# Next batch's norm, and the queries' half of its first projection and rotation, moved ahead of the second norm's columns

## The reference, cut to what matters

```python
x = x + attn(layernorm(x), Wq, Wk, Wv, Wo, lambda_*)   # x: (16, 1024, 256)
x = x + ffn(layernorm(x), ...)

def attn(x):                       # 16 half-heads of 16 columns, 8 value heads of 32
    q, k = rope(x @ Wq.T) * scaling, rope(x @ Wk.T)
    v = x @ Wv.T
    probs = softmax(einsum('bhtd,bhsd->bhts', q, k))
    diff = probs[:, :, 0] - lam * probs[:, :, 1]
    a = einsum('bhts,bhsd->bhtd', diff, v)
    a = a * rsqrt(mean(a * a) + 1e-05) * (1.0 - LAMBDA_INIT)
    return a @ Wo.T

def ffn(x):                        # a recurrence from batch to batch, c carried along
    def step(c, xt):
        ft = sigmoid(xt @ wf.T + c @ uf.T + bf)
        it = sigmoid(xt @ wi.T + c @ ui.T + bi)
        gt = tanh(xt @ wc.T + c @ uc.T + bc)
        return ft * c + it * gt
    c_final = scan(step, c0, x)
    return tanh(x @ wo.T + c_final @ uo.T + bo)
```

## Time and profile before

| what | us |
|---|---|
| median of 3 runs | 5033.72 (5031.82 to 5034.27) |
| the profiled execution, its own time | 5053.02 |
| its span, first to last instruction | 5051.2 |
| PE busy in it | 4895.6 (97%) |
| DVE busy | 3960.6 (78%) |
| POOL busy | 2930.4 (58%) |
| ACT busy | 2884.9 (57%) |

### The profile page before, as it was taken

The page is one execution under the profiler, slowest core; times in us unless marked ns, Lnnn a source line. Parts: engine busy times, 40 slices in busy tenths (PEclk is TensorE's granted clock), DMA queues, the critical chain, the costliest instruction groups (busy, mean ns, idle before and its releaser), DMA issues.

```text
span 5051.2 us, 67243 instructions
## 1 busy us (share of the span) xinstructions
PE 4895.6 (97%) x24784; PEld 1745.4 (35%) x24784; DVE 3960.6 (78%) x6295; ACT 2884.9 (57%) x5221; POOL 2930.4 (58%) x2134
## 2 busy tenths in 40 slices
PE   7999999999999999999999999999999999999999
PEld 2224242332424233242332424233242433324237
DVE  7888878888887878878887887888788787887526
ACT  1565646656465665646566464665646566564642
POOL 3583837657374674728567383764738477472740
PEclk7899999999999999999999999999999999999999
DMA  6121222303122130222313123230312313022117
GB/s 151 30 56 52 47 66 53 66 32 66 47 47 72 34 76 38 55 59 47 72 34 62 46 47 70 48 66 30 67 48 47 72 34 76 39 47 55 68 51 291
DMA packets 127867, 311.19 MB, mean 62 GB/s; under 512 B 27313, under 2 KB 30514, under 8 KB 113714
## 3 DMA queue, kind: packets, MB, share of 16 engines
q1 hardware_dynamic: 124562, 289.72, 24.1%
q10 hardware_dynamic: 2976, 17.17, 0.9%
HBM read 172.07 MB, written 99.61 MB: 54 GB/s over the span
## 4 chain that ended last, share of the span: by engine, by line
PE 77%; POOL 11%; ACT 5%; DVE 3%; issue 3%; DMA 0%; SPq 0%; ACTq 0%; DVEq 0%; POOLq 0%
PE s_ps L795 15%; PE o_ps L835 15%; PE st L822 14%; PE st L928 13%; POOL pair_sum L484 11%; PE sum_ps L850 7%; PE st L763 4%; PE st L781 4%; ACT probs L591 3%; DVE neg_max L1127 2%; PE st L1005 2%; PE st L906 1%; PE o_ps L750 1%; DVE xa L1114 1%; PE s_ps L1005 1%
## 5 line engine op out<-in xcount | busy, mean ns | idle before, releaser
L484 POOL TENSOR_TENSOR pair_sum<-probs 128x512 f32<-128x512 f32 x2048 | 2822.1, 1414 | 1211.3 <-ACT probs L591 1210.6
L1127 DVE TENSOR_REDUCE neg_max<-s_ps 128x1 f32<-128x512 f32 x4096 | 2582.1, 682 | 700.2 <-PE s_ps L795 697.8
L591 ACT ACTIVATE probs<-st 128x512 f32<-128x512 f32 x4096 | 2162.3, 603 | 971.6 <-PE st L822 810.6
L795 PE MATMUL s_ps<-k_stack,q_stack 96*128 96x512 bf16 x4096 | 1523.0, 389 | 43.5 <-DVE neg_max L1127 37.0
L822 PE MATMUL st<-q_stack,k_stack 99*128 99x512 bf16 x4096 | 1475.8, 385 | 28.7 <-ACT probs L591 7.5
L835 PE MATMUL o_ps<-probs,values 128*32 128x512 f32 x8192 | 1095.3, 607 | 12.2 <-ACT probs L591 8.5
L822 PEld LDWEIGHTS st<-q_stack,k_stack 99*128 99x128 bf16 x4096 | 368.3, 97 | 1360.1 <-ACT probs L591 905.2
L795 PEld LDWEIGHTS s_ps<-k_stack,q_stack 96*128 96x128 bf16 x4096 | 400.7, 98 | 686.0 <-DVE neg_max L1127 336.6
L850 PE MATMUL sum_ps<-pair_sum,ones 128*32 128x512 f32 x4096 | 534.9, 594 | 26.6 <-POOL pair_sum L484 26.6
L928 PE MATMUL st<-pair_sum,weights 128*128 128x512 f32 x768 | 381.9, 594 | 11.8 <-ACT pair_sum L547 11.8
L541 ACT ACTIVATE probs<-st,gate_bias 128x512 f32<-128x512 f32 x192 | 131.7, 686 | 441.7 <-PE st L928 441.7
(11 more groups left out here) (151 smaller groups left out, 2926.6 us busy)
## 6 DMA issues: line engine op xcount, KB each, us to landing
q_stack<-qk_parts SPq DMA_DIRECT2D x384, 128.0 KB, 4.3
k_stack<-qk_parts SPq DMA_DIRECT2D x381, 128.0 KB, 7.0
swapped<-xa SPq DMA_DIRECT2D x128, 256.0 KB, 2.4
qk_parts<-swapped SPq DMA_DIRECT2D x64, 512.0 KB, 2.8
qk_parts<-low_part SPq DMA_DIRECT2D x64, 256.0 KB, 3.0
probs<-in_x SPq DMA_DIRECT2D x16, 1024.0 KB, 9.7
x_rows<-probs SPq DMA_DIRECT2D x16, 1024.0 KB, 3.9
xa<-in_x SPq DMA_DIRECT2D x15, 1024.0 KB, 6.0
```

Source lines behind the costliest of these rows:

```text
L484: pool.tensor_tensor(pair_sum[q % 2][:, h, :], probs[a % 4][:, h, :], probs[(a + 1) % 4][:, h, :], ALU.add)\
L591: act.activation(probs[kk % 4][:, h, :], st[n % BANKS][:, :], ACT.Exp).then_inc(exp_done, 1)
L795: pe.matmul(s_ps[i % BANKS][:, :], q_stack[g][0:SROWS, s, t * P:(t + 1) * P], k_stack[g][0:SROWS, s, h * HALF:(h + 1) * HALF], start=True, ...
L1127: dve.tensor_reduce(neg_max2[:, at, i % 2:i % 2 + 1], s_ps[i % BANKS][:, :], AX.X, ALU.max, negate=True).then_inc(max_done, 1)
```

## The change

With "following" for a batch b < NB - 2, that is, one in whose iteration batch b+2's first unit is prepared:

- The next norm's eight `bn_stats` go from the end of the batch into steps 26 to 31 of the odd attention, the seven small operations behind its last step. POOL makes the scales before those of the second norm.
- ACT applies the norm right behind the last mean square's reciprocal root, in two halves, each with its `take_xt`. PE transposes half 0 in front of `WO` tile 2 and half 1 in front of tile 3.
- PE projects the queries (two tiles) behind `WO` tile 3 and before the first gate. ACT takes them before the second norm's columns. SP swaps them behind the store of x2 and stores the parts before `shift_rows`.
- DVE makes rotation steps 0, 1, 2, 4, 6 between the last 15 maxima of `LATE` (`ROPE_BESIDE`), behind the second norm's second half. ACT makes casts 3 and 5 in front of gates 1 and 3.
- The second norm's transposes of half 0 go in front of the third gate's cell half, and `turn_max` in front of gate 6.
- The keys' two tiles come at the end of the iteration, all eight scores beside them (1, 1, 2, 4), and only the keys' rotation is left in the even attention, in steps 1, 2, 4, 6, 9. `score_plan` counts both moves.
- Before the loop POOL rotates unit 2 as well, so the first attention has no rotation.
- The slots of the ring are counted anew. What is computed stays the same.

```diff
+FIRST_QK0, FIRST_QK1, FIRST_VAL, NEXT_QK0, PRE = 0, 4, 8, 12, 16
+QK1, WO, QK0, GATE, QK0_LAST, GEE = 0, 12, 16, 18, 30, 32
...
-ROPE_AT = ({1: 0, 2: 1, 3: 2, 4: 7, 5: 8, 6: 4, 7: 9, 9: 6, 13: 11, 16: 13},
+ROPE_AT = ({1: 7, 2: 8, 4: 9, 6: 11, 9: 13},
            {5: 0, 6: 1, 7: 2, 8: 7, 9: 8, 10: 4, 12: 9, 13: 6, 16: 11, 20: 13})
-CAST_AT = ({4: 3, 7: 5, 11: 10, 14: 12}, {9: 3, 12: 5, 14: 10, 18: 12})
+CAST_AT = ({5: 10, 7: 12}, {9: 3, 12: 5, 14: 10, 18: 12})
+ROWS_AT = {26: (0, 1), 28: (2, 3), 29: (4,), 30: (5, 6), 31: (7,)}
+ROPE_BESIDE = ((0, 1), (1, 2), (2, 5), (4, 5), (6, 2))
...
+ROW_WORK = 0.6
...
+    WORK[1][s] += ROW_WORK * len(ROWS_AT.get(s, ()))
...
@@ sync
                 if not last:
                     if b > 0:
-                        swap(u + 2, 0, ab)
-                    store_parts(u + 2)
+                        swap_part(u + 2, 1, slot(b - 1, QK0_LAST + 1))
+                        store_part(u + 2, 1)
                     stack(u + 2, 0, 0)
...
                 sp.dma_start(x2_scr[b, :, :], x2).then_inc(x2_out, 16)
+                if b < NB - 2:
+                    swap_part(u + 4, 0, slot(b, QK0 + 1))
...
+                if b < NB - 2:
+                    store_part(u + 4, 0)
+                if not last:
                     shift_rows(u + 2, 0)
...
-            swap(2, 0, act_base(0, False))
+            swap(2, NEXT_QK0)
             shift_rows(0, 0)
+            store_parts(2)
@@ gpsimd
+                if b < NB - 2:
+                    next_scales(b)
                 for h in range(2):
                     inv_sqrt_half(b, h)
-                if b < NB - 2:
-                    next_scales(b)
...
+            rope(2)
             for b in range(NB - 1):
                 iteration(b, False)
@@ scalar
+                if following:
+                    for h in range(2):
+                        normalise_next(b, range(4 * h, 4 * h + 4))
+                        take_xt(own(b) - 1, xt, (h,))
+                    take_half(0, slot(b, QK0))
+                take_xt(own(b), xt2, (0,))
+
+                casts = {(0, 0, 1): (3,), (0, 1, 0): (5,)}
...
                         for a, func in enumerate((ACT.Sigmoid, ACT.Sigmoid, ACT.Tanh)):
-                            if b < NB - 2 and (h, m, a) == (1, 1, 2):
-                                take_xt(own + 1, xt, (1,))
+                            if following:
+                                for step in casts.get((h, m, a), ()):
+                                    part_of(2 * b + 4, step)
...
                 if not last:
                     act.preload_act_table_set("natural_log_exp_and_others")
+                if following:
+                    take_half(1, slot(b, QK0_LAST))
@@ tensor
-                rows_out(WO, W_O, attn_t, b, ab, js=(2, 3))
+                if following:
+                    transposes(xa, ln1_out, b + 2, own(b) - 1, halves=(0,))
+                rows_out([slot(b, WO + 2)], W_O, attn_t, js=(2,))
+                if following:
+                    transposes(xa, ln1_out, b + 2, own(b) - 1, halves=(1,))
+                rows_out([slot(b, WO + 3)], W_O, attn_t, js=(3,))
+                if following:
+                    pe.wait_ge(xt_out, 4 * own(b))
+                    project(0, 0, slot(b, QK0))
...
                 for i in range(BANKS):
-                    turn(GATE + i, b, ab)
+                    if i == BANKS - 1:
+                        transposes(xn2, ln2_out, b, own(b), halves=(0,))
+                    turn(slot(b, GATE + i))
                     gate_part(i, True, True, False)
...
-                    if i == 5 and not last:
-                        turn_max(u + 2)
                     if i == 6:
-                        pe.wait_ge(xt_out, 4 * own + 4)
-                    if i in (9, 11) and b < NB - 2:
-                        transposes(xa, ln1_out, b + 2, own + 1, halves=(i // 11,))
+                        pe.wait_ge(xt_out, 4 * own(b) + 4)
+                        if not last:
+                            turn_max(u + 2)
...
-                if b < NB - 2:
-                    pe.wait_ge(xt_out, 4 * (own + 2))
+                if following:
+                    project(1, 0, slot(b, QK0_LAST),
+                            ((u + 3, 1, i) for i in range(BEFORE, BEFORE + BESIDE)), (1, 1, 2, 4))
+                elif not last:
+                    for i in range(BEFORE, BEFORE + BESIDE):
+                        score(u + 3, 1, i)
@@ vector
                         rope(turned, [ROPE_AT[g][s]])
+                    if following is not None and s in ROWS_AT:
+                        dve.wait_ge(x_in, 16 * (following + 1))
+                        norm_rows(xa, ROWS_AT[s])
...
-                attention(u, 0, u + 1, PLAN0, None if last else u + 2)
+                attention(u, 0, u + 1, PLAN0, u + 2 if 0 < b and not last else None)
...
-                          None if last else u + 3)
+                          None if last else u + 3, b + 2 if following else None)
+                if following:
+                    norm_stats(b + 2, -0.5)
...
-                maxima(u + 2, late, LATE[3])
                 normalise_half(b, 1, x2, xn2)
+                for step, n in ROPE_BESIDE:
+                    if following:
+                        rope(u + 4, (step,))
+                    maxima(u + 2, late, n)
                 if not last:
-                    maxima(u + 2, late, LATE[4])
                     join_max(u + 2)
-                    if b < NB - 2:
-                        dve.wait_ge(x_in, 16 * b + 48)
-                        norm_stats(b + 2, xa, -0.5)
                     split_shift(u + 2)
```

More of the change, by code:

```diff
@@ L181, in ring @@
             return st[n % BANKS][:, :]
-        tail_ps = [ring(ring_base(NB - 1, True) + GEE + j) for j in range(3)] + [s_ps[2][:, :]]
+        tail_ps = [ring(slot(NB - 1, GEE + j)) for j in range(3)] + [s_ps[2][:, :]]
         first_in = sem("first_in")
@@ L249, in build, with own @@
         block = ctx.enter_context(nc.Block())
-        def act_base(b, last):
-            return b * ACT_ITER + (PRE - (PRE if last else 0))
+        def own(b):
+            return 2 * b + (3 if b < NB - 2 else 2 if b == NB - 2 else 1)
         def flat(buffer):
@@ L275, in value, with swap_part, swap @@
                 return v if isinstance(v, int) else sp.lower_val(v)
-            def swap(u, g, ab):
-                first = isinstance(u, int) and u == 0
-                raw_out = [value(ab + (QK1 if g else QK0) + 2 * X + 2) for X in range(2)]
-                for X in range(2):
[L283 to L288, removed]
+            def swap_part(u, X, n):
+                sp.wait_ge(act_out, taken(n))
+                if u > 0:
+                    sp.wait_ge(parts_out[X], 32 * u)
+                for a in range(2):
+                    sp.dma_start(swapped[a:P:2, X, :], raw[X][1 - a:P:2, :])\
+                      .then_inc(swap_in[X], 16)
+            def swap(u, first):
+                for X in range(2):
+                    swap_part(u, X, first + 2 * X + 1)
             def store_part(u, X):
@@ L554, in take_qk, with take_v @@
                         act.wait_ge(rope_done, 2 * u - 1 + X)
[L555 to L561, removed]
+                    take_half(X, first + 2 * X)
+            def take_v(slots, js):
+                for n, j in zip(slots, js):
+                    take(n, values[:, 2 * j:2 * j + 2, :].rearrange("p a b -> p (a b)"))
             def copy_o(u, g, r):
@@ L637, in iteration @@
                     if not last and i == 2:
-                        take_v(rb, VAL, (2, 3))
-                own = 2 * b + (1 if last else 2)
-                take_xt(own, xt2, (0,))
+                        take_v([slot(b, VAL[j]) for j in (2, 3)], (2, 3))
                 def normalise_next(b, ts):
@@ L677, in take_first @@
                 act.wait_ge(rope_done, X + 1)
-                for h in range(2):
-                    take(0, QK1 + 2 * X + h, raw[X][:, h * HALF:(h + 1) * HALF])
+                take_half(X, FIRST_QK1 + 2 * X)
             for step in (3, 5):
@@ L874, in iteration @@
             def iteration(b, last):
-                ab = act_base(b, last)
                 u = 2 * b
-                if not last:
-                    if b > 0:
-                        qk(0, b, ab, ((u + 1, 1, i) for i in range(BEFORE, sum(EARLY))),
-                           (1, 1, 0, 0, 1, 1, 2, 2))
-                    pe.wait_ge(act_out, ab + QK0 + 4)
-                else:
-                    for i in range(BEFORE, sum(EARLY)):
-                        score(u + 1, 1, i)
-                    pe.wait_ge(act_out, ab + PRE)
+                following = b < NB - 2
+                pe.wait_ge(act_out, taken(slot(b, LAST_RMS[0] if last else QK1) - 1))
                 attention(u, 0, u + 1, PLAN0)
@@ L985, in _ @@
             turn_max(0)
-            for i in range(sum(EARLY)):
+            for i in range(BEFORE + BESIDE):
                 score(1, 1, i)
```

232 lines of the change are left out of this document (119 added, 113 removed).

## The result

| | us |
|---|---|
| kernel before, median of 4 | 5033.58 (5031.82 to 5034.27) |
| changed kernel, median of 4 | 5065.56 (5064.42 to 5069.43) |
| ratio | 1.0064, interval 1.0052 to 1.0076 |
| profiled execution after, its own time and span | 5069.43, 5067.6 |

The account below looks back on a forecast made before the run. PE's own work was taken to bound the kernel, so only waits that PE feels count. Terms sum to +0.15 us a batch, +2 over 14, 0 with the first batch, on 5033.7: 5033 us, range 5010 to 5056.

Parts of the forecast that it names:

- term 6: Odd attention: eight bn_stats beside POOL's additions on a busy DVE, +0.1 us a batch (-0.4 to +1.0).
- Term 1: Even attention: without five rotation steps POOL's additions no longer delay PE, -2.1 us in each of batches 1 to 14.
- Term 2: Batch's end, norm ahead of output rows: PE waits for half 1 behind ACT's copies, +1.2 us a batch.
- Term 3: First gates at batch's end: LATE's maxima held behind rotation steps on DVE, +0.45 us a batch (0 to 2.0).
- rival (b): Slower: queries' rotation on DVE holds LATE's maxima in the first gates, +1.6 us a batch, 5056 us; 15%.
- Term 4: Batch's end, gates' second halves: third gate's cell half hides the wait for copies of the second norm's columns, -0.9 us.
- Term 5: Batch's last stretch: PE waits for maxima, fourth score 1.0 us, first key tile later, +1.4 us (0.9 to 1.9).
- Hidden: Work predicted to cost PE nothing: POOL's next-norm scales, shifted second-norm columns, turn_max and cell, SP's earlier store of queries.
- the first batch: First even attention has no rotation, -2 us; POOL's 27.4 us rotation of unit 2 before the loop stays hidden.
- (a): Faster: PE's new waits at the batch's end overlap, a batch 1.6 us shorter, 5010 us; 31%.
- (c): Slower: POOL's additions stay late in the even attention's steps 1 to 9, +1.65 us a batch, 5056 us; 10%.
- (d): Slower: the 6.2 us rotation step becomes regular, one in four batches, 5 us each, 5051 us; 3%.

Follow-up runs that it names:

- e1: Changed kernel with one score of the odd attention's plan moved back from step 1 to step 2; 5030.9 us, ratio 0.9962.
- e5: Kernel before with the queries' five rotation steps in the even attention cut to 16 of 1024 columns; 5005.11 us, ratio 0.9933.
- e6: Kernel before with the queries' five even-attention rotation steps each replaced by a one-input tensor_reduce about as long; 5006.15 us, ratio 0.9936.
- e3: Changed kernel with ACT normalising all eight tiles before it copies half 0's transposed columns; 5048.86 us, ratio 1.0002.
- e4: Changed kernel with the edits of e1 and e3 together; 5014.47 us, ratio 0.9931.
- e2: Kernel before with only one score of the odd attention's plan moved from step 2 to step 1; 5083.1 us, ratio 1.0067.
- e7: Changed kernel with both edits of e4 and six instead of eight scores beside the keys' tiles; 5001.47 us, ratio 0.9926.
- a0: Changed kernel run again unaltered on another chip, as reference, against the kernel before; 5068.03 us, ratio 1.0057.

## Why the prediction was wrong

**The step that failed is term 6, the odd attention at +0.1.** That term priced the eight bn_stats and asked only whether they meet POOL. The prediction read `score_plan` for the even attention ("five more scores before step 8") and did not read what the work added for the bn_stats does to `PLAN1`: it noted "scores moved ahead" as a possible gain of POOL's. One score went over the limit of three banks just where DVE still has the sums of the unit before to finish: from its transpose at 1477.42 to the first maximum's end at about 1481.3 it is busy for 3.9 us. Measured: +2.75 a batch, against bounds of -0.4 to +1.0, and in fifteen odd attentions, not fourteen, since the same `PLAN1` serves all of them. Of the 41.3 us, about 18 are the wait (15 x 1.19, 98.47 less e1's 97.28), about 20 the lowered clock behind it, 3.6 the rest. None of the four rivals had this mechanism. With this score put back the measured stages give 5033.6 - 36.8 + 32.2 + 3.6 = 5032.6, and e1 measured 5030.9: the rest of the sum held. That it comes so near to 5033 is in part luck: the even attentions gained 5.4 us more than the sum had for them (36.8, where 14 x 2.1 + 2 is 31.4), the ends lost 2.1 more (32.2, where 14 x 2.15 is 30.1) and the odd attentions without the score 2.2 more (3.6, where 14 x 0.1 is 1.4), which nearly cancels. The batch in the stretches above is 299.1 us long, and one with a lowered clock 300.7, where the prediction had called itself wrong over 299.0.

- **Term 6's own question** was answered rightly. All bn_stats of `norm_rows` after:

```profile
L1056 DVE BATCH_NORM_STATS2 stats<-xa 128x6 f32<-128x256 f32 x128 | 48.4, 416 | 4.7 <-DMA xa<-in_x 4.6
```

  0.416 us in the mean, where e5, in which they stand in the batch's end, has 0.410. They don't meet POOL in any way that the trace shows: the 98 of its additions that overlap one took 1.26 to 1.30 us, as those beside maxima alone. Whether the remaining 0.23 us of the odd attention are theirs or those of other moved scores, no run tells.
- **Term 1**, -2.1: right in kind, measured -2.43, and nothing was late in its place. e5 and e6 show the cause of 1.98 of it, the meeting of the five steps with POOL. The other 0.45 came with what e5 and e6 leave as it was, the two casts on ACT, the places of the keys' steps and the plan of scores, and no run tells these apart.
- **Term 2**, +1.2: right. The wait is 0.96 by the row, and taking it away gave 1.18 in e3.
- **Term 3**, +0.45: 0.3 us at one score in the later batches. In the first seven DVE waits 1.4 to 3.3 us for `swapped` instead of 0.9, and there the end is 93.0 to 94.8 long instead of 92.53. Over seven batches that is 6 us. In five of the seven SP's issue of the two swaps takes 1.6 to 1.8 us instead of 1.1; in the other two, the longest among them, it is as short as later on, and the transfers land later. What the seven have in common is a packet of the instruction queue q8 beside the swap. DMA in the 5.3 us from the first swap's issue, in the longest of them and in a later batch (queue: packets, MB, share; then KB each and us to landing):

```profile
q1 hardware_dynamic: 176, 0.52, 25.6%
q8 instruction: 1, 0.02, 2.1%
...
swapped<-xa SPq DMA_DIRECT2D x2, 256.0 KB, 3.5
...
q1 hardware_dynamic: 176, 0.52, 24.8%
...
swapped<-xa SPq DMA_DIRECT2D x2, 256.0 KB, 2.3
```

  Each of the seven has such a packet of 16 KB, 0.9 to 1.9 us long, which starts between 2.3 us before the first issue and 1.9 behind it, and none of the later seven has one. e1 agrees: its first batch has neither the packet nor the delay, and its next six have both. So the delay goes with the loading of instructions; how the one holds up the other was not tested. This is the start of rival (b), which needed 0.9 us of delay everywhere.
- **Term 4**, -0.9: right, no wait is left in front of the gates' second halves.
- **Term 5**, +1.4: right. The waits of 0.94 and 0.21 us stand in the fence above; with the smaller losses between them the stretch loses 1.75 against 0.41 before, +1.34.
- **Hidden, and the first batch**, -2: right. POOL's `rope` ahead of the loop, first and last row of its timeline, and the first addition:

```profile
126.44 2.35 POOL L474 TENSOR_TENSOR xa<-xa,rope_tab 128x1024 f32<-128x1024 f32 x1 [19.63 <-DMA swapped<-xa]
...
154.01 2.12 POOL L490 TENSOR_TENSOR low_part<-xa,swapped 128x1024 bf16<-128x1024 f32 x1 [2.49 <-DMA qk_parts<-low_part]
169.01 3.72 POOL L505 TENSOR_TENSOR pair_sum<-probs 128x512 f32<-128x512 f32 x3 [12.88 <-ACT probs L615]
```

  It ends at 156.1 with 12.9 us to spare. The first even attention went from 98.87 to 96.55.
- **Rivals.** (a) did not come of itself: terms 3 and 5 did not shrink; e4 reaches its size only through e3. (c) falls with term 1, (d) with the row of L1139: no step over 2.33 us.
- **How the base stood.** That the long steps of the earlier trace rows are missing from the median's runs held for the chip of the first measurement. On the chip of e1 to e4 the kernel before took 5040 to 5063, and e2's profiled execution has them again, up to 6.205 us. None is in the changed kernel, e1, e3, e4 or e7, nor in e5 and e6, where the queries' part never met POOL. So the change also removes a scatter; what starts such a step was not found. Of the four in the trace before, three were followed by a lowered clock, the first at 1408.90 behind the step at 1400.24, and those even attentions are 5.0 to 5.8 us longer; the one without it is 3.5 us longer.

## What to carry to other kernels

When a change feeds a hand-written planner that rounds, print the plan before and after it and read every entry that moved, not only those near the change. Where a work queue is limited by banks, the first item beyond the limit waits for the first result of the consumer: find the places where that consumer is late, and keep that item behind them. A short wait of PE is to be priced with the clock that may follow it: here a wait of 1.62 us cost 2.5 us on average (37.7 over fifteen).

## What was not expected of the hardware

- A wait of 1.62 us on PE, in a stream otherwise dense, was followed in 12 of 15 batches by a stretch at 1.2 GHz. It cost 1.6 us (100.1 less 98.47), as much again as the wait, and 3.0 us once, in the batch whose stretch from 1481.40 to 1487.90 reads 0.50. In a0 and e3 it was again 12 of 15, in e2 9 of 15. In the six kernels without this wait (before, e1, e4, e5, e6, e7) none of the first fifteen odd attentions starts with a lowered clock. The waits of about 1 us at the batch's end were followed by none in any of the first fourteen batches. In e2 the same wait of 1.62 us at 1487.77 was followed by the full clock, so the wait's length alone does not decide.
- A DVE instruction with two SBUF inputs, 1.23 us by itself, can stand for 6.2 us beside POOL's back-to-back additions, and whether it does varies from run to run and from chip to chip. A reduction of the same 1024 columns stayed at 1.205 to 1.211 in all 75 cases.
